# A routed expert layer behind an attention layer: GpSimd's stores in pairs, and three pieces of work in another place

## The chip, the core and the metric

The kernel runs on one core of a Trainium2 chip. A core has five engines that run their own instruction streams and meet only at semaphores: TensorE (PE; PEld is its weight load), VectorE (DVE), ScalarE (ACT), GpSimd (POOL) and SyncE (SP). The metric is the device time of one execution, in microseconds. The kernel before takes 296.75 us, the median of 3 runs (296.5 to 297.4).

## The reference

Eight sequences of 512 tokens (4096 tokens, width 256) pass through two gated layers, in fp32:

```python
x = x + tanh(g_xattn) * attention(layernorm(x), ctx)     # 16 heads, 16x16 scores within each token
x = x + tanh(g_ffn)   * ffn(layernorm(x))
# ffn: logits = xf @ Wg + bg ; idx = argmax(softmax(logits))
#      h = gelu(xf @ W1[idx] + b1[idx]) ; out = h @ W2[idx] + b2[idx]    (8 experts, width 256)
```

Each token's row goes through exactly one of 8 experts, so the kernel sorts the rows by expert.

## The kernel before

**Attention.** The 4096 tokens are 32 tiles of 128 rows, worked in 16 pairs (`pairs`). Each `slot(k, ...)` is one pair: projections, scores, softmax, values and output on TensorE, with VectorE and ScalarE between. Two pairs are a batch of four tiles; `m` numbers the batches, `last_batch` is 7.

**Routing.** When a batch's rows are final (`residual`, `stats_1`, `stats_2` on VectorE, then the standard deviation's power `pow_x1` on GpSimd), VectorE picks each row's expert (`pick_1` to `pick_7`), TensorE counts ranks by small matmuls (`ranks`), VectorE turns ranks into row numbers (`read_ranks`, `place_1` to `place_3`; the last of them casts to `pos_i`), and GpSimd scatters the four tiles to `routed_rows` in DRAM by four indirect DMAs (`route_tile`, line 1409; below: *routes*). 16 pairs are 32 routes on the semaphore `routed`, 16 counts each.

**Experts.** The sorted rows are read back in 39 blocks (`blocks`) of 128 rows. Block b passes, on every engine in order of b:

- SP `fetch`: reads the block's first row from a table, then loads it (`xb_in`), into a ring of 8; it waits until block b - 8 is finished. Blocks 0 to 15 (`EARLY`) hold rows of the batches placed first and come from a first table; blocks from 16 on need the second table (`tab_1` to `tab_10` on VectorE, spread over blocks 5 to 10) and all 32 routes (`routed`).
- VectorE `norm_b` (L1116), three blocks ahead; TensorE `transpose_b` (L640), two blocks ahead; ScalarE `copy_xbt` (L805) and the copy of the expert's first weights `copy_w1` (L790); TensorE `layer1` (L650, out to `ps_so` for even and `ps_tr` for odd blocks); ScalarE `gelu` (L798); TensorE `layer2` (L669, out to `ps_av` or `ps_to`); VectorE `finish` (L1133 adds the bias, frees the bank by `yb_done`; L1137 makes the output rows, `yf_done`); GpSimd `store` (L1465, an indirect DMA to `out_rows`, into a ring of 8 output tiles, semaphores `stored0` to `stored7`).
- The last three blocks (`AHEAD`) have the part of the output that doesn't need TensorE made beforehand (`prepare`, L1146) and then one instruction each (`finish_ahead`, L1157; two halves for the very last).

TensorE's slot for block b is `layer1(b)`, `layer2(b - 1)`, `transpose_b(b + 2)`.

**The seam.** While the last batch is still being routed, the first blocks already run. The order is written out by hand. On GpSimd: the two routes of batch 6, `pow_x1(15)`, the other two, the stores of blocks 0 to 2, two routes of batch 7, the store of block 3, two routes, and then only stores. On VectorE `end()` places batch 6 around the last `residual`; `pick_1(7)` waits for `pow_x1(15)`, and what stands behind it (the `finish` of block 1) waits too. On TensorE `ranks(7)` stands behind `layer2(4)`.

```python
def store(b, q, turn):
    ...
        wait_apart(pool, yf_done, b + 1, passed_pool)
    pool.indirect_dma_start(out, ... yf[j], None, bounds_check=limit, ...).then_inc(stored[j], 16)
```

A GpSimd wait holds back all that stands behind it on GpSimd; the instruction stream before has no wait there for an indirect DMA's landing.

## Time and profile before

| | |
|---|---|
| median of 3 runs | 296.75 us (296.5 to 297.4) |
| the profiled execution's own time | 295.98 us |
| its span, first to last instruction | 294.1 us |
| PE busy over the span | 277.9 us (94%) |
| DVE / ACT / POOL busy | 210.4 / 103.8 / 129.4 us |
| chain that ended last | PE 87%, DVE 3%, issue 2%, another core or an unknown queue 2% |
| indirect DMAs: routes, stores | 32, 39 |

The busy time of an engine is a sum over stages with different limits, so a change in one stage is read from that stage's rows. In the timelines a row is a start, a duration, the engine, the source line, the operation, what it writes and reads, and in square brackets the idle time of the engine before it with what ended it; "remote" there is a releaser that the profile does not tell. A POOL row of an indirect DMA is the time in which GpSimd makes its descriptors, not the transfer.

### The profile page before, as it was taken

What the parts mean: (1) busy time and instruction counts of PE and PEld (TensorE: products, weight loads), DVE (VectorE), ACT (ScalarE), POOL (GpSimd) and SP (SyncE); (2) the same over time, 40 slices, a digit from 0 to 9 for tenths busy, and PEclk for the clock granted to TensorE, in tenths of its full rate; (3) what the DMA queues carried; (4) which work ended last, traced back from release to release, by engine and by line L of the source; (5) the groups of instructions that cost most, each with busy time, mean ns of one, the idle gap of its engine ahead of it and who ended that gap; (6) DMA issues with size and microseconds to landing.
All of it is one profiled execution on the core that took longest, in us unless ns stands there. A gap on an engine that the chain in (4) does not pass through costs nothing.

```text
span 294.1 us, 9791 instructions
## 1 busy us (share of the span) xinstructions
PE 277.9 (94%) x3185; PEld 220.9 (75%) x3186; DVE 210.4 (72%) x613; ACT 103.8 (35%) x258; POOL 129.4 (44%) x156
## 2 busy tenths in 40 slices
PE   7999999999999999999999999899874799999994
PEld 6667777677677776776777768679763699999993
DVE  7667668786796786786877788698653666666664
ACT  2120321311303213113031131267451577777761
POOL 9613132152543624525427245413747254455455
PEclk9999999999999999999999999999999699999999
DMA  7866345476575764765746634332444244433410
GB/s 235 281 165 160 83 125 154 122 211 178 171 200 141 212 187 143 223 174 174 225 122 214 202 89 123 98 92 61 120 131 141 77 143 132 115 111 118 131 70 23
DMA packets 31240, 43.22 MB, mean 147 GB/s; under 512 B 7661, under 2 KB 18542, under 8 KB 31216
## 3 DMA queue, kind: packets, MB, share of 16 engines
q1 hardware_dynamic: 17760, 21.35, 26.7%
q10 hardware_dynamic: 10048, 12.99, 15.2%
q0 software_dynamic: 3408, 8.59, 8.2%
q8 instruction: 11, 0.18, 0.3%
q14 instruction: 13, 0.11, 0.1%
HBM read 24.83 MB, written 10.60 MB: 120 GB/s over the span
## 4 chain that ended last, share of the span: by engine, by line
PE 87%; DVE 3%; issue 2%; another core or an unknown queue 2%; DMA 2%; POOL 1%; ACT 1%; DVEq 0%; ACTq 0%; SPq 0%; POOLq 0%
PE ps_pr L409 18%; PE ps_qo L438 18%; PE ps_av L483 11%; PE ps_so L464 9%; PE ps_so L650 6%; PE ps_tr L650 5%; PE ps_to L669 5%; PE ps_av L669 5%; PE ps_tr L473 3%; PE ps_pr L640 3%; PE ps_to L496 2%; DMA sb_wqg<-wqg_in 2%; PE ps_pr L438 1%; PE ps_to L430 1%
## 5 line engine op out<-in xcount | busy, mean ns | idle before, releaser
L409 PE MATMUL ps_pr<-sb_wkv,sb_ct 128*128 128x512 f32 x120 | 57.7, 604 | 0.0
L723 ACT ACTIVATE sb_pe_x<-sb_pe_x 128x512 f32<-128x512 f32 x16 | 10.1, 631 | 111.5 <-DVE sb_pe_x L899 103.5
L1409 POOL DMA_INDIRECT routed_rows<-sb_xs,sb_pos_i x32 | 32.5, 1017 | 15.4 <-DVE sb_pos_i L1008 7.7
L1395 POOL TENSOR_SCALAR sb_ve<-sb_mv 128x2 f32<-128x2 f32 x16 | 3.5, 221 | 78.4 <-DVE sb_mv L858 75.9
L409 PEld LDWEIGHTS ps_pr<-sb_wkv,sb_ct 128*128 128x128 f32 x120 | 20.5, 190 | 17.7 <-issue 17.4
L483 PE MATMUL ps_av<-sb_vb,sb_at 128*32 128x128 f32 x1024 | 32.2, 274 | 1.1 <-issue 1.1
L464 PE MATMUL ps_so<-sb_kb,sb_y_q 128*32 128x128 f32 x1024 | 31.2, 273 | 0.1
L483 PEld LDWEIGHTS ps_av<-sb_vb,sb_at 128*32 128x32 f32 x1024 | 27.2, 110 | 5.0 <-issue 4.9
L438 PE MATMUL ps_qo<-sb_wog,sb_ot 128*128 128x264 f32 x120 | 29.6, 388 | 0.0
L438 PEld LDWEIGHTS ps_qo<-sb_wog,sb_ot 128*128 128x128 f32 x120 | 22.5, 190 | 9.2 <-issue 6.4
L438 PE MATMUL ps_qo<-sb_wqg_c,sb_xt 128*128 128x264 f32 x120 | 29.3, 387 | 0.0
L464 PEld LDWEIGHTS ps_so<-sb_kb,sb_y_q 128*32 128x32 f32 x1024 | 28.0, 110 | 1.6 <-issue 1.1
L790 ACT COPY sb_kb<-sb_w_all 128x514 f32 x39 | 24.2, 622 | 12.7 <-issue 12.7
L884 DVE STREAM_TRANSPOSE sb_y_q<-sb_q_n 128x512 f32<-128x512 f32 x16 | 17.4, 1091 | 15.6 <-ACT sb_q_n L718 15.6
L302 POOL TENSOR_TENSOR sb_cn<-sb_om,sb_rt 128x512 f32<-128x512 f32 x14 | 18.0, 1286 | 20.3 <-DVE sb_om L923 20.3
L1465 POOL DMA_INDIRECT out_rows<-sb_y_k,sb_tok_i x20 | 19.7, 983 | 16.3 <-issue 8.4
L650 PE MATMUL ps_so<-sb_ct,sb_kb 128*128 128x128 f32 x160 | 22.3, 284 | 4.4 <-ACT sb_ct L805 4.4
L438 PEld LDWEIGHTS ps_qo<-sb_wqg_c,sb_xt 128*128 128x128 f32 x120 | 21.7, 190 | 3.8 <-issue 0.5
L650 PEld LDWEIGHTS ps_so<-sb_ct,sb_kb 128*128 128x128 f32 x160 | 20.3, 198 | 4.9 <-issue 4.4
L669 PE MATMUL ps_to<-sb_w,sb_ht 128*128 x76 | 20.7, 397 | 2.5 <-DVE sb_yo L1133 1.3
L669 PE MATMUL ps_av<-sb_w,sb_ht 128*128 x80 | 20.4, 378 | 2.5 <-issue 2.0
L650 PE MATMUL ps_tr<-sb_ct,sb_kb 128*128 128x128 f32 x152 | 20.2, 276 | 0.0
(158 smaller groups left out, 493.9 us busy)
## 6 DMA issues: line engine op xcount, KB each, us to landing
sb_x<-x_in ACTq DMA_DIRECT2D x16, 256.0 KB, 3.5
sb_kb<-sb_y_k SPq DMA_DIRECT2D x124, 32.0 KB
sb_vb<-sb_y_v SPq DMA_DIRECT2D x120, 32.0 KB
sb_ct<-ctx_in ACTq DMA_DIRECT2D x14, 256.0 KB, 3.2
sb_xt<-xt_in_ ACTq DMA_DIRECT2D x14, 256.0 KB, 4.3
sb_xb<-routed_rows SPq DMA_DIRECT2D x25, 134.0 KB
sb_w_all<-w_in_ SPq DMA_DIRECT2D x4, 514.0 KB
sb_w<-w_in SPq DMA_DIRECT2D x4, 512.0 KB
```

The source lines that it names most:

```text
L302: eng.tensor_tensor(cn[:].rearrange("p u h i -> p h u i"), om[:].rearrange("p h (u i) -> p h u i", u=2), rt[:].rearrange("p (u i) -> p u i ...
L409: last = pe.matmul(pr[:, s * 512:(s + 1) * 512], lhsT=ct[i][:, kc, s, :], rhs=wkv[:, :, kc, :], start=(kc == 0), stop=(kc == KC - 1))
L438: last = pe.matmul(dst[:, s * 512:s * 512 + DE], lhsT=src[:, kc, s, :], rhs=w[:, kc, :], start=(kc == 0), stop=(kc == KC - 1))
L464: last = pe.matmul(so[32 * q:32 * q + 32, r * P:(r + 1) * P], lhsT=y_q[:, 4 * q + r, u:u + 2, :].rearrange("p a b -> p (a b)"), rhs=kb[i][ ...
L483: last = pe.matmul(av[32 * q:32 * q + 32, r * P:(r + 1) * P], lhsT=at[:, 4 * r + q, u:u + 2, :].rearrange("p a b -> p (a b)"), rhs=vb[i][: ...
L650: last = pe.matmul(h_ps[i][:, ic * P:(ic + 1) * P], lhsT=w1_sb[q % W1_RING][:, kc * D + ic * P:kc * D + (ic + 1) * P], rhs=xbt[i][:, kc, : ...
L669: last = pe.matmul(dst, lhsT=ht[i][:, ic, :], rhs=w2_sb[:, bass.ds(ex, 1), ic, first:end].rearrange("p a d -> p (a d)"), start=(ic == 0), ...
L723: act.activation(pe_x[:], pe_x[:], ACT.Exp, scale=float(H) ** -0.5).then_inc(exp_done, 1)
L790: act.copy(w1_sb[q % W1_RING], w1_all[:, bass.ds(ex, 1), :].rearrange("p a f -> p (a f)")).then_inc(w1_done, 1)
L884: dve.transpose(y_q[:, :, 0:3:2, :].rearrange("p a u i -> p i u a"), q_n[:].rearrange("p s (h i) -> p i s h", h=H)).then_inc(yq_out, 1)
L1409: pool.indirect_dma_start(rows, bass.IndirectOffsetOnAxis(ap=row_numbers(batch)[:, c:c + 1], axis=0), rows_of(j)[:, s, :], None).then_inc( ...
L1465: pool.indirect_dma_start(out, bass.IndirectOffsetOnAxis(ap=tok_i[j][:, 0:1], axis=0), yf[j], None, bounds_check=limit, oob_is_err=False). ...
```

## The change

Five edits. (1) GpSimd: all four routes of batch 7 stand behind the store of block 3, with a wait for `routed` behind the second and the fourth; behind the store of every other odd block up to 35 GpSimd waits until the store before it has landed. (2) VectorE: `place_2` and `place_3` of batch 6 stand ahead of the last `residual`. (3) TensorE: `ranks(7)` stands ahead of `layer2(4)`. (4) VectorE: `prepare` of the last block stands right behind that of block 36, in a buffer of its own (`y_q`). (5) TensorE: blocks 2 to 15 are written out and blocks 16 to 31 run in a loop of 8, where there were two loops of 4; the small matmul for `lap_ps` follows block 14 instead of 13.

```diff
+YL_ORDER = (0, 2, 1)
...
             slots(pe, pre, slot, end)
-            def slots_4(first, turns):
-
-                with pe.Fori(0, turns) as turn:
-                    for k in range(first, first + W1_RING):
-                        expert_slot(W1_RING * turn + k, k % W1_RING, turn)
-
-            for b in range(2, 6):
+            for b in range(2, EARLY):
                 if b == 5:
                     layer1(5, 5, 0)
-                    layer2(4, 0)
                     pe.wait_ge(res_step, 3 * last_pair + 1)
                     ranks(last_batch)
+                    layer2(4, 0)
                     transpose_b(7, 1)
                 else:
                     expert_slot(b, b % RING, b // RING)
-            slots_4(6, 2)
-            pe.wait_ge(lap_done, 1)
-            pe.matmul(lap_ps, lhsT=ones[:], rhs=lap_d[:], start=True, stop=True).then_inc(lap_spread, 1)
-            slots_4(14, 5)
-            for b in range(34, blocks + 1):
-                expert_slot(b, b % RING, b // RING)
+                if b == RING + 6:
+                    pe.wait_ge(lap_done, 1)
+                    pe.matmul(lap_ps, lhsT=ones[:], rhs=lap_d[:], start=True, stop=True).then_inc(lap_spread, 1)
+            block_slots(pe, expert_slot, 1)
...
+            def yl(b):
+
+                return y_q[:].rearrange("p a b h -> p (a b h)")[:, 0:D] if b == blocks - 1 else yo[b % 2][:]
+
             def prepare(b):
...
-                dve.wait_ge(yf_done, b - 1)
+                if b < blocks - 1:
+                    dve.wait_ge(yf_done, b - 1)
                 dve.wait_ge(stored[j], 16 * (b // OUT))
-                dve.scalar_tensor_tensor(yo[i][:], b2_sb[...
+                dve.scalar_tensor_tensor(yl(b), b2_sb[...
...
             def finish_ahead(b):
...
-                dve.wait_ge(yl_done, b - (blocks - AHEAD) + 1)
+                dve.wait_ge(yl_done, YL_ORDER.index(b - (blocks - AHEAD)) + 1)
...
                 place_1(m)
+                place_2(m)
+                place_3(m)
                 residual(n + 1, (n + 1) % 4)
-                place_2(m)
                 stats_1(n + 1, (n + 1) % 4)
-                place_3(m)
                 stats_2(n + 1, (n + 1) % 4)
...
-                if known and blocks - AHEAD <= b < blocks:
+                if known and blocks - AHEAD <= b < blocks - 1:
                     prepare(b)
+                if known and b == blocks - AHEAD:
+                    prepare(blocks - 1)
...
             for b in range(EARLY):
                 store(b, b % RING, b // RING)
-                if b in (2, 3):
-                    route_nth(last_batch, 2 * b - 4)
-                    route_nth(last_batch, 2 * b - 3)
-            block_slots(pool, store, 0)
+                if b == 3:
+                    for i in range(4):
+                        route_nth(last_batch, i)
+                        if i % 2 == 1:
+                            pool.wait_ge(routed, 32 * pairs - 16 * (3 - i))
+                elif b % 2 == 1:
+                    pool.wait_ge(stored[(b - 1) % OUT], 16 * ((b - 1) // OUT + 1))
+            def store_in_twos(b, q, turn):
+                store(b, q, turn)
+                if isinstance(b, int) and b >= blocks - 3:
+                    return
+                if q % 2 == 1 and isinstance(b, int):
+                    pool.wait_ge(stored[q - 1], 16 * (turn + 1))
+                elif q % 2 == 1:
+                    wait_apart(pool, stored[q - 1], 16 * (turn + 1), passed_pool)
+
+            block_slots(pool, store_in_twos, 0)
```

The first place is GpSimd's stream at the seam. `routed_rows` DMAs are routes (from `sb_xs_0` batch 6, from `sb_xs_1` batch 7), `out_rows` DMAs are stores; the number at the end of `sb_tok_i` is the block. Before:

```order
L1409 DMA routed_rows<-sb_xs_0,sb_pos_i 33792x268 x2
L1465 DMA out_rows<-sb_y_k_0,sb_tok_i_0 4096x256 [waits yf_done]
L1465 DMA out_rows<-sb_y_k_0,sb_tok_i_1 4096x256 [waits yf_done]
L1465 DMA out_rows<-sb_q_n,sb_tok_i_2 4096x256 [waits yf_done]
L1409 DMA routed_rows<-sb_xs_1,sb_pos_i 33792x268 [waits pos_done]
L1409 DMA routed_rows<-sb_xs_1,sb_pos_i 33792x268
L1465 DMA out_rows<-sb_q_n,sb_tok_i_3 4096x256 [waits yf_done]
L1409 DMA routed_rows<-sb_xs_1,sb_pos_i 33792x268 x2
```

And after:

```order
L1411 DMA routed_rows<-sb_xs_0,sb_pos_i 33792x268 x2
L1467 DMA out_rows<-sb_y_k_0,sb_tok_i_0 4096x256 [waits yf_done]
L1467 DMA out_rows<-sb_y_k_0,sb_tok_i_1 4096x256 [waits yf_done]
L1467 DMA out_rows<-sb_q_n,sb_tok_i_2 4096x256 [waits stored0,yf_done]
L1467 DMA out_rows<-sb_q_n,sb_tok_i_3 4096x256 [waits yf_done]
L1411 DMA routed_rows<-sb_xs_1,sb_pos_i 33792x268 [waits pos_done]
L1411 DMA routed_rows<-sb_xs_1,sb_pos_i 33792x268
L1411 DMA routed_rows<-sb_xs_1,sb_pos_i 33792x268 [waits routed]
L1411 DMA routed_rows<-sb_xs_1,sb_pos_i 33792x268
L1467 DMA out_rows<-sb_y_k_1,sb_tok_i_4 4096x256 [waits routed,yf_done]
L1467 DMA out_rows<-sb_y_k_1,sb_tok_i_5 4096x256 [waits yf_done]
L1467 DMA out_rows<-sb_y_v_0,sb_tok_i_6 4096x256 [waits stored4,yf_done]
```

The store of block 3 has moved ahead of batch 7's routes, and waits on landings (`stored0`, `routed`, `stored4`) stand where there were none; no wait stands between the store of block 3 and the first two routes but the old one on `pos_done`.

The second place is the end of `end()` on VectorE. L992 to L1008 are `read_ranks` to `place_3` of batch 6, L934 is the last residual, L940 and L946 its statistics. Before:

```order
L992 TENSOR_TENSOR sb_rb<-ps_av,sb_base 128x32
L997 TENSOR_TENSOR sb_base<-ps_av,sb_base 128x8
L998 TENSOR_TENSOR sb_rb<-sb_rb,sb_oh_b 128x32
L934 SCALAR_TENSOR_TENSOR sb_xs<-ps_qo,sb_tg,sb_x 128x2x264
L1002 TENSOR_REDUCE sb_pos<-sb_rb 128x4
L940 BN_STATS sb_st<-sb_xs 128x6 x2
L1008 CAST sb_pos_i<-sb_pos 128x4
L946 BN_AGGR sb_xs<-sb_st 128x2 x2
```

And after:

```order
L987 TENSOR_TENSOR sb_rb<-ps_av,sb_base 128x32
L992 TENSOR_TENSOR sb_base<-ps_av,sb_base 128x8
L993 TENSOR_TENSOR sb_rb<-sb_rb,sb_oh_b 128x32
L997 TENSOR_REDUCE sb_pos<-sb_rb 128x4
L1003 CAST sb_pos_i<-sb_pos 128x4
L929 SCALAR_TENSOR_TENSOR sb_xs<-ps_qo,sb_tg,sb_x 128x2x264
L935 BN_STATS sb_st<-sb_xs 128x6 x2
L941 BN_AGGR sb_xs<-sb_st 128x2 x2
```

The cast that GpSimd's first two routes wait for no longer stands behind the residual.

The third place is the last three blocks on VectorE, from the output rows of block 35 (`sb_q_n`). Before:

```order
L1137 SCALAR_TENSOR_TENSOR sb_q_n<-sb_yo,sb_tg,sb_xb 128x256
L1143 TENSOR_LOAD sb_tab
L1143 ISA x2
L1146 ISA
L1146 SCALAR_TENSOR_TENSOR sb_yo<-sb_b,sb_tg,sb_xb 128x256
L1148 TENSOR_TENSOR sb_tok_i<-sb_xb,sb_skip 128x1
L1157 SCALAR_TENSOR_TENSOR sb_y_k<-ps_av,sb_tg,sb_yo 128x256
L1143 TENSOR_LOAD sb_tab
```

And after:

```order
L1132 SCALAR_TENSOR_TENSOR sb_q_n<-sb_yo,sb_tg,sb_xb 128x256
L1142 TENSOR_LOAD sb_tab
L1142 ISA x2
L1146 ISA
L1146 SCALAR_TENSOR_TENSOR sb_yo<-sb_b,sb_tg,sb_xb 128x256
L1148 TENSOR_TENSOR sb_tok_i<-sb_xb,sb_skip 128x1
L1142 TENSOR_LOAD sb_tab
L1142 ISA x2
L1146 ISA
L1146 SCALAR_TENSOR_TENSOR sb_y_q<-sb_b,sb_tg,sb_wkv 128x256
L1148 TENSOR_TENSOR sb_tok_i<-sb_wkv,sb_skip 128x1
L1157 SCALAR_TENSOR_TENSOR sb_y_k<-ps_av,sb_tg,sb_yo 128x256
```

One whole `prepare` (a register load from the table, two computing instructions) has moved ahead of the output rows of block 36 (L1157).

## Rows read from the trace of the kernel before

**Rows 1.** Busy us by stretch: PE, PEld, DVE, ACT, POOL; PEclk, DMA share, GB/s
```profile
203.00:215.00 12.00, 9.64 (x72) 8.58 (x70) 7.75 (x32) 6.18 (x16) 8.00 (x9) 1.00 0.34 104
215.00:225.00 10.00, 7.34 (x45) 6.33 (x46) 6.88 (x31) 4.45 (x12) 5.83 (x6) 1.00 0.46 137
225.00:235.00 10.00, 5.87 (x28) 5.04 (x27) 4.46 (x17) 3.52 (x10) 3.96 (x5) 0.66 0.24 79
...
245.00:285.00 40.00, 40.00 (x283) 36.84 (x282) 25.33 (x80) 30.58 (x82) 19.96 (x21) 1.00 0.38 114
```

**Rows 2.** Timeline of GpSimd at the seam: start, us, what
```profile
204.88 1.07 POOL L1409 DMA_INDIRECT routed_rows<-sb_xs,sb_pos_i  x1 [4.75 <-DVE sb_pos_i L1008]
...
208.49 1.07 POOL L1409 DMA_INDIRECT routed_rows<-sb_xs,sb_pos_i  x1 [0.19 <-issue]
...
213.73 0.98 POOL L1465 DMA_INDIRECT out_rows<-sb_q_n,sb_tok_i  x1 [0.30 <-issue]
217.65 0.97 POOL L1409 DMA_INDIRECT routed_rows<-sb_xs,sb_pos_i  x1 [2.94 <-DVE sb_pos_i L1008]
...
226.63 0.98 POOL L1465 DMA_INDIRECT out_rows<-sb_y_v,sb_tok_i  x1 [0.30 <-issue]
```

**Rows 3.** Timeline of TensorE at the seam
```profile
209.58 1.13 PE L669 MATMUL ps_to<-sb_w,sb_ht 128*128 x4 [1.33 <-DVE sb_yo L1133]
...
212.55 0.24 PE L536 MATMUL ps_qo<-sb_oh_b,sb_ones 128*128 128x32 bf16 x4
...
215.13 1.12 PE L669 MATMUL ps_to<-sb_w,sb_ht 128*128 x4 [1.16 <-issue]
...
220.11 1.03 PE L669 MATMUL ps_to<-sb_w,sb_ht 128*128 x4
220.97 0.38 PE L640 MATMUL ps_pr<-sb_cst,sb_ct 128*128 128x128 f32 x2
...
229.75 2.07 PE L650 MATMUL ps_so<-sb_ct,sb_kb 128*128 128x128 f32 x8 [4.13 <-ACT sb_ct L805]
```

**Rows 4.** Timeline of VectorE at the seam
```profile
201.67 0.18 DVE L998 TENSOR_TENSOR sb_rb<-sb_rb,sb_oh_b 128x32 f32<-128x32 f32 x1
...
203.90 0.15 DVE L1008 CAST sb_pos_i<-sb_pos 128x4 uint32<-128x4 f32 x1
...
208.33 0.19 DVE L958 TENSOR_TENSOR sb_lg<-sb_xs 128x32 f32<-128x32 f32 x1 [2.29 <-POOL sb_xs L1404]
...
211.85 0.19 DVE L987 TENSOR_TENSOR sb_oh_b<-sb_le,sb_lw 128x32 bf16<-128x32 f32 x1
...
215.90 0.19 DVE L992 TENSOR_TENSOR sb_rb<-ps_qo,sb_base 128x32 f32<-128x32 f32 x1 [2.69 <-remote]
...
229.30 0.42 DVE L1133 TENSOR_TENSOR sb_yo<-ps_to,sb_b 128x256 f32<-128x256 f32 x1 [5.93 <-remote]
...
232.85 0.20 DVE L1080 CAST sb_tab<-sb_tab_t 128x64 int32<-128x64 f32 x1
```

**Rows 5.** Timeline of ScalarE at the seam
```profile
229.25 0.37 ACT L805 COPY sb_ct<-ps_pr 128x256 f32<-128x256 f32 x1 [5.11 <-remote]
```

**Rows 6.** Chain of waits, steady stretch: start, us, what (two `transpose_b`)
```profile
259.53 0.22 PE ps_pr L640 x2
...
261.50 0.22 PE ps_pr L640 x2
```

**Rows 7.** Timeline of all engines at the end
```profile
287.61 0.48 DVE L1157 SCALAR_TENSOR_TENSOR sb_y_k<-ps_av,sb_tg,sb_yo 128x256 f32<-128x256 f32 x1
...
288.37 0.98 POOL L1465 DMA_INDIRECT out_rows<-sb_y_k,sb_tok_i  x1 [0.63 <-DVE sb_y_k L1157]
...
290.07 0.48 DVE L1146 SCALAR_TENSOR_TENSOR sb_yo<-sb_b,sb_tg,sb_wkv 128x256 f32<-128x256 f32 x1 [0.36 <-DVE sb_y_k L1157]
...
290.86 0.34 DVE L1157 SCALAR_TENSOR_TENSOR sb_y_v<-ps_tr,sb_tg,sb_yo 128x128 f32<-128x128 f32 x1
291.47 0.98 POOL L1465 DMA_INDIRECT out_rows<-sb_y_v,sb_tok_i  x1 [0.51 <-DVE sb_y_v L1157]
```

More of the change, by code:

```diff
@@ L1137, in finish @@
                 dve.scalar_tensor_tensor(yf[j], yo[i][:], tg[:, 1:2], xb[q][:, 0:D], ALU.mult, ALU.add).then_inc(yf_done, 1)
+            def yl(b):
+                return y_q[:].rearrange("p a b h -> p (a b h)")[:, 0:D] if b == blocks - 1 else yo[b % 2][:]
             def prepare(b):
-                i, j = b % 2, b % OUT
+                j = b % OUT
                 x_b = xb[b % RING]
                 ex = dve.value_load(tab[0:1, 1, b:b + 1], min_val=0, max_val=E - 1)
-                dve.wait_ge(yf_done, b - 1)
+                if b < blocks - 1:
+                    dve.wait_ge(yf_done, b - 1)
                 dve.wait_ge(stored[j], 16 * (b // OUT))
-                dve.scalar_tensor_tensor(yo[i][:], b2_sb[:, bass.ds(ex, 1), :].rearrange("p a d -> p (a d)"), tg[:, 1:2],
+                dve.scalar_tensor_tensor(yl(b), b2_sb[:, bass.ds(ex, 1), :].rearrange("p a d -> p (a d)"), tg[:, 1:2],
                                          x_b[:, 0:D], ALU.mult, ALU.add).then_inc(yl_done, 1)
@@ L1156, in finish_ahead @@
                     dve.wait_ge(y_done, b + nth + 1)
-                    last = dve.scalar_tensor_tensor(yf[j][:, first:end], src, tg[:, 1:2], yo[i][:, first:end], ALU.mult, ALU.add)
+                    last = dve.scalar_tensor_tensor(yf[j][:, first:end], src, tg[:, 1:2], yl(b)[:, first:end], ALU.mult, ALU.add)
                 last.then_inc(yf_done, 1)
```

## The prediction, made blind

> **What bounds the kernel now.** I read the busy time by stretch first, to see where TensorE, the bound of most of the span, is not busy; then the timelines of the engines at that place; then the chain of waits; then the end.
>
> From 245 to 285 us TensorE is busy for 40.00 of 40.00 us, at the full clock [rows 1]. A block costs it 1.97 us there, from one transposition to the next (261.50 - 259.53) [rows 6]. Nothing done to other engines in that stretch can bring anything. The stretch from 203 to 235 us is another matter: TensorE is idle for 2.36, 2.66 and 4.13 us of its three parts, 9.15 us in all, and in the last part its mean clock is 0.66, that is, part of it at the lower of its two levels, 1.2 GHz, after the long idle time [rows 1]. (1 - 0.66) x 10 x 2 = 6.8 us of it were at half clock. I put 4.0 of them behind 229.75, where TensorE works again (layer 1 of block 10 takes 2.07 us [rows 3], more than a whole block in the steady stretch): work of 2.0 us that takes 4.0, another 2.0 us. So the seam loses 11.1 us, and 285.6 us would be the time without any of it (296.75 - 11.1). The reader is to see three separate losses in it.
>
> *Loss 1, 1.33 us.* Layer 2 of block 3 starts at 209.58, released by VectorE's bias addition [rows 3]. That one stood behind `pick_1(7)`, which waited 2.29 us for GpSimd's power (208.33) [rows 4], which stood behind two routes that started at 204.88 [rows 2], 0.83 us after their row numbers were cast (203.90 + 0.15) [rows 4]. The cast stood behind the last residual.
>
> *Loss 2, about 1.7 us.* TensorE finished the ranks of batch 7 at 212.79 by its rows [rows 3], but VectorE, which had waited 2.69 us for them, read them at 215.90 [rows 4]. TensorE itself waited 1.16 us at 215.13 [rows 3] for a gelu that was late in the same way, and some 0.5 us a slot later.
>
> *Loss 3, 8.2 us.* It is the same thing, larger. Layer 2 of block 7 was done at 221.14 and the transposition of block 10 at 221.35 [rows 3], but VectorE went on with the one at 229.30 and ScalarE with the other at 229.25, after idle times of 5.93 and 5.11 us that end with "remote" [rows 4, 5]. TensorE had nothing more it could do and stood 4.13 us until 229.75 [rows 3]; the rest of the idle time (9.15 - 1.33 - 1.16 - 0.5 - 4.13 = 2.0 us) was at block 8 in the same stretch, and the 2.0 us of half clock belong to it.
>
> So in losses 2 and 3 TensorE's work was done and its announcements reached the others 3 and 8 us late. What stands beside both is GpSimd: from 208.49 to 214.71 it issued 5 indirect DMAs, and from 217.65 to 227.61 8 of them, 0.30 us apart [rows 2]. In the steady stretch there are 21 of them in 40 us [rows 1], one a block, with about 1 us between, and TensorE never waits. I take the dense issue for the cause. The rows show that the two go together, not how.
>
> **The change part by part.**
>
> *Row numbers ahead of the last residual.* `place_2` can start at 201.85, when L998 is done [rows 4], and the cast ends about 0.4 us later, at 202.25, in a gap in which VectorE waits for TensorE anyway; 1.80 us earlier than 204.05. The routes start at 203.1, the power ends at 206.5 instead of 208.3 and so does the wait of `pick_1(7)`. Layer 2 of block 3 can then follow its predecessor at 208.25: the 1.33 us go, with 0.5 us to spare. Bounds: 0 (something else late there) to 1.8. I take 1.3.
>
> *Ranks ahead of layer 2 of block 4.* Removed from their way is one layer 2, 0.87 us. Added is a wait: one-hot rows were ready at 212.04 (211.85 + 0.19) [rows 4], and layer 1 of block 5 was done at about 211.7 (212.55 less a layer 2 [rows 3]), so TensorE would wait 0.35 us, with layer 2, its store and all later blocks behind it; the five small matmuls cost 0.1 us in either place. With the previous edit VectorE is 1.2 us earlier at this point, and the wait shrinks. Bounds: -0.5 to +0.1 us; I take -0.1.
>
> *Waits on GpSimd.* The last store is issued at 291.47 [rows 7], and the span ends at 294.1: an indirect DMA lands at most 2.63 us after its start. Two issues take 0.98 + 0.30 + 0.98 = 2.26 us, so the wait for the first of a pair costs at most 0.4 us by itself. But GpSimd then starts again only after 0.28 us (VectorE's rows at 288.09, the store at 288.37) [rows 7] to 0.83 us (above). A pair takes up to 2.63 + 0.83 = 3.46 us, with a pause of 0.6 to 1.2 us, where it took 2.56 with 0.30. Two blocks take TensorE 3.94 us: in the steady stretch the wait is free. Behind batch 7's routes the second of each pair is waited for too, a pause of 2.63 - 0.98 + 0.83 = 2.5 us, twice. The eight DMAs of loss 3 thereby become pairs: at the most two in a row. I expect that TensorE's announcements pass in the pauses, as they did around the pair at 204.88.
>
> What stays dense: routes 3 and 4 of batch 6 and the stores of blocks 0 and 1 are still four in a row, and so are the stores of blocks 2 and 3 with the first two routes of batch 7, if their row numbers are there. So I leave loss 2 as it is (0; bounds +1.7, all gone, and -1.7, doubled), and of loss 3 leave one stall of 2.0 us, the size of loss 2: 8.2 - 2.0 = 6.2 us gained, bounds 0 and 8.2.
>
> What is late next: batch 7's routes. With the numbers 4 us earlier (ranks not held up for 3 us, 1.3 from the first edit) the last one is issued about 222 and landed about 224.5; SP's fetch of block 16 then waits for it. Unheld, block 16 reaches TensorE's layer 1 at about 231 (12 slots of 1.97 behind block 4, in whose slot layer 2 of block 3 stands at 208.25) and must be normalised by 228: it is covered by 3 us, if the table, cast at 232.85 [rows 4] behind loss 3, comes some 8 us earlier, as all of VectorE does. The stores run late by up to 9 us then and gain 0.5 us a pair on TensorE; 8 output tiles allow 8 x 1.97 = 15.8 us less the landing.
>
> A page of the Trainium skill speaks of the price of such a wait: "DMA: Bandwidth & Descriptors", section "Anatomy of one DMA", has about 2.0 us of fixed time for a GpSimd DMA plus bytes over 436 GB/s, an estimate of 2.3 us for 128 rows of 1 KB. By it a wait for the first of a pair would be over as the second is issued, and the pause would be the restart alone.
>
> *The last block's preparation ahead.* One `prepare` moves ahead of block 36's output rows. It takes about 1.3 us of VectorE's path (register load, 0.48 and 0.15 us). From 286 us VectorE is nearly dense, so block 36's rows come about 1.0 us later than 288.09, and those of the last block, which today wait for the preparation at 290.07 [rows 7], gain at most 0.55 us. GpSimd then has three stores to issue 1.28 us apart: 289.1 + 0.27 + 2 x 1.28 = 291.9 instead of 291.47. A loss of 0.4 us; bounds -0.8 to +0.5.
>
> *Loops.* TensorE runs the same matmuls; 16 slots instead of 28 run in a loop. Steady slots with and without a branch cost 1.97 us, so 0.
>
> Sum: 1.3 - 0.1 + 0 + 6.2 - 0.4 = 7.0 us. The sum is made in the profiled execution, 295.98 us (294.1 of span and 1.9 around it), which stands 0.8 us under the median; the losses are differences and carry over. 296.75 - 7.0 = 289.7 us.
>
> **The rivals.**
>
> *A, all of losses 2 and 3 goes.* The pauses let every announcement through. For it: no late one in 40 us of steady issue. Against: four in a row remain twice. 289.7 - 1.7 - 2.0 = 286.0 us.
>
> *B, the pauses do nothing.* What holds TensorE's announcements is the number of DMAs worked off, not their spacing, or something else at that place. For it: the rows show no mechanism. Then only the first and the small terms are left: 296.75 - 1.3 + 0.1 + 0.4 = 295.95, within a measurement of no change.
>
> *C, slower: held until GpSimd has caught up.* If announcements are held for as long as GpSimd has indirect DMAs waiting, the pauses lengthen the hold. Batch 7's group was 8 x 1.28 = 10.2 us long; in pairs, with the store of block 3 ahead, it is 1.3 + 3.46 + 3.46 + 3.46 + 1.0 = 12.7 us. TensorE stands 2.5 us longer, at half clock after it: 295.95 + 2.5 = 298.5 us. It decides if TensorE still idles when GpSimd is between pairs.
>
> *D, the loop, not the pauses.* TensorE's 4.13 us begin where it branches back to block 10, and end with ScalarE's copy [rows 3]; against it, the branches between 245 and 285 us cost nothing [rows 1]. Gone with its half clock, 4.1 + 2.0, and the other terms as in B: 295.95 - 6.1 = 289.85 us. The Trainium skill ("Runtime: NRT & Kernel Launch", section "Instruction fetch mechanics") says that a taken branch out of the fetched window waits for a fetch; by that rule the gap would be one. The trace agrees neither in the steady branches nor in what ended the gap.
>
> **How the numbers follow.** Forecast (287.5 to 292.5 us): 0.44. A: 0.17. B: 0.18. C: 0.16. D: 0.05. The range reaches from 285.0, where A would lie with a better end, to 297.8, which leaves out most of C and little else. A measurement of this kernel can tell about 0.3%, 0.9 us, from no change. Faster: forecast, A, D and a small part of B, 0.69; same: the rest of B, 0.14; slower: C and a little of B, 0.17.
>
> **What would show each step.** First edit: GpSimd's first route of the group at about 203.1, and layer 2 of block 3 without idle time before it. Ranks: at most 0.5 us of wait ahead of them. Pauses: gaps of 0.6 us and more behind every second store at the seam, no idle time of VectorE or ScalarE over 3 us that ends with "remote", and TensorE's clock at 1.00 from 225 to 235. End: the store of block 36 later, the last one not earlier. The forecast is wrong if those idle times are still there although GpSimd pauses (B, C), or if SP waits for `routed` while TensorE idles at block 16.

## The result, and the profile after

The changed kernel takes 291.62 us (median of 6 runs, 290.77 to 293.15), the kernel before 296.84 us beside it (6 runs, 296.07 to 297.4): a ratio of 0.9837, 95% interval 0.9816 to 0.9859. The forecast was 289.7 us: right in direction and within the range, 1.9 us too low. The profiled execution took 290.77 us (span 288.9). Later sets of runs add what no single chip shows: on two of the four chips that they ran on, no trace has the losses 2 and 3 that the change goes for. Here and below a time is the median of all runs of a kernel and a ratio is that of its fast runs alone, so the two differ a little where slow ones fell in (1 to 3 of the runs with pauses to block 15, with threes, and with edit 2 or edit 4 undone).

The busy times by stretch, as [rows 1] (PE, PEld, DVE, ACT, POOL busy, PE's clock, DMA share, GB/s):

```profile
203.00:215.00 12.00, 11.03 (x81) 9.92 (x80) 9.41 (x38) 7.90 (x21) 7.99 (x9) 1.00 0.39 115
215.00:225.00 10.00, 8.23 (x56) 7.20 (x56) 7.65 (x34) 5.53 (x16) 4.94 (x5) 1.00 0.43 137
225.00:235.00 10.00, 10.00 (x73) 9.23 (x73) 7.52 (x27) 7.35 (x21) 6.20 (x6) 1.00 0.43 124
```

TensorE idles for 2.7 us of this stretch instead of 9.15, and is never at its lower clock. GpSimd's timeline answers to [rows 2]:

```profile
202.75 1.07 POOL L1411 DMA_INDIRECT routed_rows<-sb_xs,sb_pos_i  x1 [3.06 <-DVE sb_pos_i L1003]
...
210.54 0.99 POOL L1467 DMA_INDIRECT out_rows<-sb_y_k,sb_tok_i  x1 [0.30 <-issue]
213.72 0.98 POOL L1467 DMA_INDIRECT out_rows<-sb_q_n,sb_tok_i  x1 [2.19 <-DMA out_rows<-sb_y_k,sb_tok_i]
215.01 0.99 POOL L1467 DMA_INDIRECT out_rows<-sb_q_n,sb_tok_i  x1 [0.30 <-issue]
216.30 0.97 POOL L1411 DMA_INDIRECT routed_rows<-sb_xs,sb_pos_i  x1 [0.30 <-issue]
217.57 0.96 POOL L1411 DMA_INDIRECT routed_rows<-sb_xs,sb_pos_i  x1 [0.30 <-issue]
220.31 1.06 POOL L1411 DMA_INDIRECT routed_rows<-sb_xs,sb_pos_i  x1 [1.77 <-DMA routed_rows<-sb_xs,sb_pos_i]
221.68 0.96 POOL L1411 DMA_INDIRECT routed_rows<-sb_xs,sb_pos_i  x1 [0.31 <-issue]
225.05 0.99 POOL L1467 DMA_INDIRECT out_rows<-sb_y_k,sb_tok_i  x1 [2.41 <-DVE sb_y_k L1132]
...
278.33 0.98 POOL L1467 DMA_INDIRECT out_rows<-sb_y_k,sb_tok_i  x1 [1.08 <-issue]
```

The pauses are there. Two of them (2.19 and 1.77 us) follow four DMAs in a row. The row of 225.05 names VectorE as what ended the pause, but that release was long past; the wait for the fourth route is behind it. TensorE's, VectorE's and ScalarE's rows answer to [rows 3 to 5]:

```profile
207.73 1.09 PE L670 MATMUL ps_to<-sb_w,sb_ht 128*128 x4
...
210.29 0.18 PE L535 MATMUL ps_qo<-sb_oh_b,sb_tri 128*128 128x40 bf16 x1 [0.36 <-DVE sb_oh_b L982]
...
219.96 1.16 PE L651 MATMUL ps_tr<-sb_ct,sb_kb 128*128 128x128 f32 x8 [1.34 <-ACT sb_ct L800]
```

```profile
212.62 0.19 DVE L987 TENSOR_TENSOR sb_rb<-ps_qo,sb_base 128x32 f32<-128x32 f32 x1 [0.97 <-remote]
```

```profile
210.91 0.37 ACT L800 COPY sb_ct<-ps_pr 128x256 f32<-128x256 f32 x1 [2.09 <-remote]
```

Layer 2 of block 3 has no idle time ahead of it, the ranks waited 0.36 us, and the longest idle time that ends with "remote" is 2.09 us where 5.93 stood. Lateness is left behind the second four in a row, though no row calls it remote: the transposition of 218.23 ends at 218.61, ScalarE copies it at 219.54, and TensorE waits 1.34 us for that copy (the row of 219.96). What is new is the end, which answers to [rows 7]:

```profile
280.51 0.48 DVE L1157 SCALAR_TENSOR_TENSOR sb_y_k<-ps_av,sb_tg,sb_yo 128x256 f32<-128x256 f32 x1
...
281.02 0.98 POOL L1467 DMA_INDIRECT out_rows<-sb_q_n,sb_tok_i  x1 [0.42 <-DMA out_rows<-sb_y_k,sb_tok_i]
...
281.82 0.61 PE L670 MATMUL ps_tr<-sb_w,sb_ht 128*128 x4
...
283.70 0.98 POOL L1467 DMA_INDIRECT out_rows<-sb_y_k,sb_tok_i  x1 [0.41 <-DMA out_rows<-sb_q_n,sb_tok_i]
...
285.62 0.35 DVE L1157 SCALAR_TENSOR_TENSOR sb_y_v<-ps_tr,sb_tg,sb_y_q 128x128 f32<-128x128 f32 x1 [1.03 <-remote]
286.27 0.98 POOL L1467 DMA_INDIRECT out_rows<-sb_y_v,sb_tok_i  x1 [0.31 <-issue]
```

The rows of block 36 are made at 280.99, but GpSimd issues their store at 283.70, 2.71 us later: it is still behind. It issues its last seven stores with pauses of at most 0.42 us, from 278.33 on, and TensorE's last announcement (the semaphore update that tells the others that its matmuls are done) is late again: its matmuls end at 282.43, and VectorE reads them at 285.62. The last store itself follows GpSimd's own store before it (0.31 us, "issue"); the rows that it stores are made at 285.97, just in time for it. In the kernel before, TensorE's last matmuls were these:

```profile
289.60 0.61 PE L669 MATMUL ps_tr<-sb_w,sb_ht 128*128 x4
```

So TensorE was through 290.21 - 282.43 = 7.8 us earlier, and from there to the last store it took 3.84 us instead of 1.26.

### The profile page after: what moved, and what is told of

The parts are those of the page before. It is cut to its first block, busy times and chain, and to the rows that moved or that the text cites. A ratio compares the mean times of both kernels' runs of the same rounds, so it can differ in the third digit from the quotient of the medians.

```text
span 288.9 us, 9745 instructions
## 1 busy us (share of the span) xinstructions
PE 275.6 (95%) x3185; PEld 219.2 (76%) x3186; DVE 211.3 (73%) x613; ACT 102.9 (36%) x258; POOL 130.4 (45%) x156
## 4 chain that ended last, share of the span: by engine, by line
PE 75%; issue 7%; POOL 5%; DVE 5%; DMA 5%; ACTq 1%; ACT 1%; POOLq 0%; DVEq 0%
PE ps_qo L439 18%; PE ps_pr L410 18%; PE ps_av L484 11%; PE ps_so L465 9%; POOL out_rows L1467 5%; PE ps_av L670 3%; PE ps_so L651 3%; PE ps_to L670 3%; PE ps_tr L474 3%; PE ps_tr L651 3%; PE ps_to L497 2%; PE ps_pr L641 2%; DMA sb_kb<-sb_y_k 2%; DMA out_rows<-sb_q_n,sb_tok_i 2%; DVE sb_kb L1279 1%
## 5 line engine op out<-in xcount | busy, mean ns | idle before, releaser
L1411 POOL DMA_INDIRECT routed_rows<-sb_xs,sb_pos_i x32 | 32.7, 1023 | 12.5 <-issue 7.4
L651 PE MATMUL ps_so<-sb_ct,sb_kb 128*128 128x128 f32 x160 | 21.2, 276 | 0.2 <-ACT sb_ct L800 0.2
L670 PE MATMUL ps_to<-sb_w,sb_ht 128*128 x76 | 20.0, 385 | 0.3 <-ACT sb_ht L793 0.2
L651 PEld LDWEIGHTS ps_so<-sb_ct,sb_kb 128*128 128x128 f32 x160 | 19.5, 192 | 0.5 <-ACT sb_ct L800 0.5
```

The lines of the kernel that those rows point to most:

```text
L651: last = pe.matmul(h_ps[i][:, ic * P:(ic + 1) * P], lhsT=w1_sb[q % W1_RING][:, kc * D + ic * P:kc * D + (ic + 1) * P], rhs=xbt[i][:, kc, : ...
L670: last = pe.matmul(dst, lhsT=ht[i][:, ic, :], rhs=w2_sb[:, bass.ds(ex, 1), ic, first:end].rearrange("p a d -> p (a d)"), start=(ic == 0), ...
L1411: pool.indirect_dma_start(rows, bass.IndirectOffsetOnAxis(ap=row_numbers(batch)[:, c:c + 1], axis=0), rows_of(j)[:, s, :], None).then_inc( ...
```

## The experiments

Each set of kernels ran on one chip beside the kernel before: the first four on chip A, the next four on chip C, two on chip B, the last two on chip D. Before took 296.2 us on A and 296.3 on B, but 283.7 on C and 284.0 on D. Times are compared within a set only, 5 rounds each (3 for the fourth). The chip of the first set, that of the result above, is not on record. No trace of the kernel before was kept on B, C or D: what is said of it there rests on its time and on the traces of the others.

| kernel | chip | us | ratio to before (95%) |
|---|---|---|---|
| pauses alone | A | 293.96 | 0.9915 (0.9881 to 0.9948) |
| loops alone | A | 296.41 | 1.0003 (0.9980 to 1.0025) |
| pauses to block 15 only | A | 295.78 | 0.9980 (0.9948 to 1.0011) |
| before, one store held | A | 303.23 | 1.0225 (1.0180 to 1.0270) |
| threes from block 16 | C | 287.84 | 1.0149 (1.0103 to 1.0195) |
| gaps, no waits | C | 283.92 | 1.0002 (0.9985 to 1.0018) |
| changed, edit 2 undone | C | 293.55 | 1.0308 (1.0252 to 1.0363) |
| changed, edit 4 undone | C | 291.07 | 1.0198 (1.0141 to 1.0254) |
| changed kernel again | B | 291.53 | 0.9833 (0.9804 to 0.9863) |
| gaps, again | B | 293.41 | 0.9894 (0.9863 to 0.9925) |
| changed, waits written out | D | 284.03 | 1.0020 (0.9996 to 1.0043) |
| changed, edit 1 undone | D | 283.01 | 0.9977 (0.9958 to 0.9995) |

**Pauses alone (edit 1).** 

> The kernel before with the first edit alone (GpSimd's routes of batch 7 behind the store of block 3, and its waits). Theory, the dense issue on GpSimd makes TensorE's announcements late: most of the gain is here, no idle time over 3 us that ends with remote; the first loss (1.3 us ahead of layer 2 of block 3) stays, so 292.5 to 293.5 us, and the stores end late as in the changed kernel. Rival, the loop: the branch at block 10 is still there, so TensorE stands 4 us at it and the time is 296 to 297 us.

```diff
-                if b in (2, 3):
-                    route_nth(last_batch, 2 * b - 4)
-                    route_nth(last_batch, 2 * b - 3)
-            block_slots(pool, store, 0)
+                if b == 3:
...
+                            pool.wait_ge(routed, 32 * pairs - 16 * (3 - i))
+                elif b % 2 == 1:
+                    pool.wait_ge(stored[(b - 1) % OUT], 16 * ((b - 1) // OUT + 1))
...
+            block_slots(pool, store_in_twos, 0)
```

293.96 us, 0.5 us above the expected range, with 225 to 235 us fully busy at the full clock, although TensorE's loop and its branch are as before. The loop is out. But GpSimd is the bound at the end, more than in the changed kernel: TensorE's last matmuls start at 283.17 and end at 283.78, and the last store starts 6.39 us later, at 290.17. Its first route had started 6.03 us behind the start of the power ahead of it (205.92 - 199.89), 4.26 us in the changed kernel (202.75 - 198.49).

```profile
199.89 0.48 POOL L1402 TENSOR_SCALAR sb_ve<-sb_xs 128x2 f32<-128x2 f32 x1 [2.72 <-DVE sb_xs L946]
...
205.92 1.07 POOL L1409 DMA_INDIRECT routed_rows<-sb_xs,sb_pos_i  x1 [4.74 <-DVE sb_pos_i L1008]
...
290.17 0.98 POOL L1465 DMA_INDIRECT out_rows<-sb_y_v,sb_tok_i  x1 [0.30 <-issue]
```

**Loops alone (edit 5).** 

> The kernel before with the fifth edit alone (TensorE's blocks 2 to 15 written out, the rest in a loop of 8; the ranks where they were). Theory of the dense issue: nothing, 296.1 to 297.5 us, with the idle times of 5 us in VectorE and ScalarE still there. Rival, the loop: they are gone, 290 to 291 us.

```diff
-            for b in range(2, 6):
+            for b in range(2, EARLY):
...
-            slots_4(6, 2)
...
-            slots_4(14, 5)
...
+            block_slots(pe, expert_slot, 1)
```

No difference, and the gap with its half clock is where it was. The edit is worth nothing, and the rule of the Trainium skill on branches ("Runtime: NRT & Kernel Launch", section "Instruction fetch mechanics") doesn't explain the gap.

```profile
225.00:235.00 10.00, 5.07 (x25) 4.71 (x26) 4.55 (x17) 3.82 (x11) 4.41 (x5) 0.66 0.29 92
```

**Pauses to block 15 only.** 

> The changed kernel without the waits behind the stores from block 16 on; those at the seam stay. GpSimd is about 9 us late there and now issues 1.28 us apart until it has caught up, some 13 stores or more, in a stretch in which TensorE was busy throughout. Theory, dense issue anywhere: TensorE stands 2 us or more between 232 and 260 us, and the 2.3 us that GpSimd's lateness costs at the end come back: about 293 us (290 to 296). Rival, only the place (the routes, the seam) makes announcements late: TensorE stays busy, and the end is earlier: 289.2 us.

```diff
-            block_slots(pool, store_in_twos, 0)
+            block_slots(pool, store, 0)
```

295.78 us: nearly all of the gain is lost, and no difference from before is left that is clear of noise. GpSimd, late from the seam, issues seven stores in a row, the first 1.52 us and the others 1.28 us ahead of the next, and the stall of the seam stands in the middle of the steady stretch (GpSimd, ScalarE, VectorE and TensorE in one timeline):

```profile
250.12 0.98 POOL L1467 DMA_INDIRECT out_rows<-sb_y_k,sb_tok_i  x1 [0.31 <-issue]
...
256.54 0.98 POOL L1467 DMA_INDIRECT out_rows<-sb_y_v,sb_tok_i  x1 [0.30 <-issue]
258.78 0.62 ACT L793 ACTIVATE sb_ht<-ps_so,sb_kb 128x128 f32<-128x128 f32 x2 [4.45 <-remote]
258.97 0.42 DVE L1128 TENSOR_TENSOR sb_yo<-ps_to,sb_b 128x256 f32<-128x256 f32 x1 [5.16 <-remote]
...
259.54 2.07 PE L670 MATMUL ps_av<-sb_w,sb_ht 128*128 x4 [5.02 <-ACT sb_ht L793]
```

**One store held in the steady stretch.** 

> The kernel before, with GpSimd's store of block 19 held until the output rows of block 22 are made, and its blocks from 16 on written out. GpSimd is then three to four blocks late in the middle of the steady stretch and issues about 9 stores 1.28 us apart. Theory, dense issue anywhere: TensorE stands 2 to 8 us between 262 and 285 us, where it was busy throughout, and the time is 299 to 305 us. Rival, only the place or the routes: nothing, 296.1 to 297.5 us.

```diff
-            block_slots(pool, store, 0)
+            for b in range(EARLY, blocks):
+                if b == 19:
+                    pool.wait_ge(yf_done, 23)
+                store(b, b % RING, b // RING)
```

303.23 us, 7.0 us slower. This is the kernel before with one added wait on GpSimd, no route near, and GpSimd's stores from block 16 on written out. It isn't a lack of output tiles: block 24, whose rows VectorE makes at 268.26, behind the stall, uses the tile of block 16, which was stored before the hold. Five dense stores later TensorE stands, at the place where [rows 1] have 40.00 of 40.00:

```profile
261.89 0.98 POOL L1465 DMA_INDIRECT out_rows<-sb_q_n,sb_tok_i  x1 [7.39 <-DVE sb_y_v L1137]
...
267.03 0.98 POOL L1465 DMA_INDIRECT out_rows<-sb_y_v,sb_tok_i  x1 [0.30 <-issue]
...
269.46 2.08 PE L650 MATMUL ps_tr<-sb_ct,sb_kb 128*128 128x128 f32 x8 [2.56 <-issue]
```

```profile
265.00:275.00 10.00, 7.44 (x33) 6.33 (x32) 3.90 (x12) 4.08 (x12) 4.57 (x6) 0.68 0.29 93
```

Dense issue on GpSimd is thereby shown as the cause, on chip A, and the place doesn't matter. That lateness of GpSimd alone doesn't do it is shown by the pauses, with which GpSimd is late too (8.0 us at block 16 in the changed kernel: rows at 240.12, store at 248.13) and TensorE goes on.

**Threes, and gaps in place of waits, on chip C.** 

> The changed kernel, with GpSimd waiting behind every third store from block 16 on (places 2, 5 and 7 of each eight) instead of every second. Theory, the end is bound by GpSimd's lateness and three in a row are few enough: 8 blocks take GpSimd about 14 us where pairs take 15.2 and TensorE 15.8, so it is some 2 us less late at the end: 290.0 us (289 to 291). Rival, three in a row already hold TensorE's announcements long enough: TensorE idles over 1 us somewhere between 235 and 275 us, and the time is 292 us or more.

```diff
-                if q % 2 == 1 and isinstance(b, int):
+                if q in (2, 5, 7) and isinstance(b, int):
```

> The changed kernel, in which GpSimd doesn't wait for landings behind the stores from block 4 on but writes 256 values a partition behind each (about 0.3 us), with the blocks from 16 on written out; the waits at the routes stay. The stores are then about 1.6 us apart without ever waiting for one to land. Theory, the spacing is what matters and 0.6 us between two is enough: no idle time over 2 us that ends with remote, GpSimd is in time at the end, 289 to 290.5 us. Rival, it is the landing that lets the announcements through (a train of DMAs of any such spacing holds them): TensorE idles 2 us or more once between 225 and 260 us, 294 to 297 us.

```diff
+            def gap(b):
+                if b > 4:
+                    pool.wait_ge(gap_done, b - 4)
+                pool.memset(vb[1][:].rearrange("p t f -> p (t f)")[:, 0:256], 0.0).then_inc(gap_done, 1)
...
+                if b >= 4:
+                    gap(b)
+            for b in range(EARLY, blocks):
+                store(b, b % RING, b // RING)
+                if b < blocks - 3:
+                    gap(b)
```

Neither question was answered, since this chip has nothing to tell them apart: before takes 283.7 us, and no row from 150 us on in the traces of the four kernels run here shows an idle time that ends with "remote", four DMAs in a row or not. The gaps cost nothing (283.92). The threes cost 1.5%: with the waits GpSimd issues its last store 5.8 us behind the end of TensorE's matmuls (283.62 - 277.84), for no gain.

**Edit 2 and edit 4 undone, on chip C.** 

> The changed kernel without the second edit (place_2 and place_3 of batch 6 behind the last residual again). Theory, GpSimd's chain of work from its routes of batch 6 to the last store sets the end: all of it is 1.3 to 1.8 us later, 292.9 to 293.4 us. Rival, the edit's worth is TensorE's loss ahead of layer 2 of block 3, and that is hidden behind GpSimd's lateness at the end: 291.6 us, no difference.

```diff
-                place_2(m)
-                place_3(m)
                 residual(n + 1, (n + 1) % 4)
+                place_2(m)
                 stats_1(n + 1, (n + 1) % 4)
+                place_3(m)
```

> The changed kernel without the fourth edit (the last block is prepared right ahead of its own output rows again). Theory, VectorE is not on the path at the end, since GpSimd issues the store of block 36 only 2.7 us after its rows are made: no difference, 291.2 to 292.0 us. Rival, the last block's rows wait for the preparation as before the change: 0.4 to 0.6 us slower.

```diff
-YL_ORDER = (0, 2, 1)
+YL_ORDER = (0, 1, 2)
...
-                if known and b == blocks - AHEAD:
-                    prepare(blocks - 1)
```

293.55 and 291.07 us. The expected numbers were for a chip like A; here both must be read against 283.7. The second shows the end most plainly. TensorE is through at 277.88 (first row; PE busy 10.00 of 10.00 in each stretch from 215 to 275 us), and GpSimd goes on until its last store at 286.73, 8.9 us later:

```profile
277.27 0.61 PE L670 MATMUL ps_tr<-sb_w,sb_ht 128*128 x4
...
286.73 0.98 POOL L1464 DMA_INDIRECT out_rows<-sb_y_v,sb_tok_i  x1 [0.30 <-issue]
```

With the waits GpSimd alone sets the time there. It gets so late that VectorE waits for output tiles (1.48 us at 240.75, ended by a store's landing). Which of the two edits is worth more isn't shown. The ratios are 1.1% apart, but their intervals touch (from 1.0252, up to 1.0254), and the changed kernel itself was not run on this chip. Nor do the traces show the 1.8 us by which edit 2 starts GpSimd earlier: from the start of the power to the store of block 4 it takes 28.4 us without the edit (224.89 - 196.50) and 28.6 us with it (226.29 - 197.68), since GpSimd then waits 3.95 us for the landing of the last route with the edit, and 2.42 us without it.

**The changed kernel and the gaps, on chip B.** 

> The changed kernel itself, in another set. The kernel before took 296.2 to 296.8 us in two sets and 283.7 us in the third, so a set's chip decides whether announcements come late. Where before takes 296 us: 291.6 us again. Where it takes 284 us: TensorE has nothing to lose there, and the waits make GpSimd 7 us late at the end, as with the preparation back in its place: 290 to 292 us, 2% slower than before. Rival, the third set's kernels were slow for the parts taken back in them, not for the waits: 284 us there.

> The kernel with a gap of 0.5 us or more behind each store in place of the waits, in another set. Where before takes 296 us: by the theory that the spacing of 1.5 us is enough, 288 to 289 us, with GpSimd in time from about block 28 on; by the rival that announcements pass only where GpSimd waits for a landing, TensorE idles 2 us or more between 225 and 260 us, 293 to 297 us. Where before takes 284 us: 283.9 us again.

Chip B is like A: before 296.3, the changed kernel 291.53 as the first time. The gaps bring 1.1% where the waits bring 1.7%; the 288 to 289 us of the theory that 1.5 us between two starts is enough are missed. The rival isn't right either, since from 242 us on no announcement is late, though GpSimd waits for no landing. With a store every 1.48 us TensorE's announcements are late twice more behind the seam, while GpSimd is in time at the end:

```profile
229.70 0.98 POOL L1468 DMA_INDIRECT out_rows<-sb_y_v,sb_tok_i  x1 [0.17 <-issue]
230.67 0.34 POOL L1476 MEMSET sb_vb<- 128x256 f32 x1
231.18 0.98 POOL L1468 DMA_INDIRECT out_rows<-sb_y_v,sb_tok_i  x1 [0.17 <-issue]
...
233.45 0.42 DVE L1129 TENSOR_TENSOR sb_yo<-ps_to,sb_b 128x256 f32<-128x256 f32 x1 [3.32 <-remote]
...
240.28 0.42 DVE L1129 TENSOR_TENSOR sb_yo<-ps_to,sb_b 128x256 f32<-128x256 f32 x1 [3.05 <-remote]
```

So 0.5 us between two stores is too little there, and 1 us (the steady stretch of before) enough. Pairs with 0.9 us and more behind them are nearly enough: in the changed kernel's first trace TensorE is idle for 0.35 us between 235 and 265 us (9.74, 10.00 and 9.91 of 10.00).

**Waits written out, and no waits, on chip D.** 

> The changed kernel with GpSimd's blocks from 16 on written out, so that its waits are on constants; the waits are the same. In the kernel whose stores were held, written-out stores followed their rows by 0.3 us, looped ones by 0.8. Where before takes 296 us: each pair is 0.5 us shorter, GpSimd is in time for the last blocks and the late announcements there go too: 288.9 us (288 to 290). Rival, the shorter pauses let less through, and TensorE idles over 1 us behind 235 us: 291 to 294 us. Where before takes 284 us: GpSimd ends 2 to 4 us late instead of 7: 286 to 288 us, still slower than before.

```diff
-            block_slots(pool, store_in_twos, 0)
+            for b in range(EARLY, blocks):
+                store_in_twos(b, b % RING, b // RING)
```

> The changed kernel with the first edit undone (GpSimd's order as before, no waits), so edits two to five alone. Where before takes 296 us: only the first loss goes, the idle times that end with remote stay: 295.2 us (294.5 to 296.3). Where before takes 284 us: no announcement is late, and the two moves on VectorE and TensorE are all that counts: 282.5 us (282 to 283.3), the best there. Rival to both: the moves bring nothing without the waits, the same time as before.

```diff
-                if b == 3:
-                    for i in range(4):
...
+                if b in (2, 3):
+                    route_nth(last_batch, 2 * b - 4)
+                    route_nth(last_batch, 2 * b - 3)
+            block_slots(pool, store, 0)
```

Chip D is like C. Written out, the same waits cost nothing clear of noise (284.03), better than I expected: from 250 us on the idle time behind most pairs is 0.3 to 0.8 us (once 1.03; 0.42 in the second row below), and GpSimd, as late as in the other kernels at block 16, is nearly in time at the end.

```profile
269.60 0.98 POOL L1467 DMA_INDIRECT out_rows<-sb_y_v,sb_tok_i  x1 [0.30 <-DVE sb_y_k L1132]
271.00 1.23 POOL L1467 DMA_INDIRECT out_rows<-sb_y_k,sb_tok_i  x1 [0.42 <-DMA out_rows<-sb_y_v,sb_tok_i]
```

Without any waits, edits 2 to 5 bring 0.2% (0.05 to 0.4%), the best kernel on this chip. Its trace is the counterpart of the held store: 19 indirect DMAs in a row, none over 0.33 us behind the one before it, and TensorE doesn't notice:

```profile
204.46 1.07 POOL L1411 DMA_INDIRECT routed_rows<-sb_xs,sb_pos_i  x1 [0.19 <-issue]
...
227.89 0.98 POOL L1467 DMA_INDIRECT out_rows<-sb_y_k,sb_tok_i  x1 [0.33 <-issue]
```

```profile
215.00:225.00 10.00, 10.00 (x74) 9.24 (x73) 8.83 (x38) 7.47 (x20) 7.83 (x8) 1.00 0.56 176
225.00:235.00 10.00, 10.00 (x74) 9.23 (x73) 6.42 (x22) 7.59 (x20) 5.88 (x6) 1.00 0.53 161
```

## Why the prediction was right, and where it was off

*The cause.* "I take the dense issue for the cause" was an inference from two things side by side. The held store shows it (chip A, +7.0 us), and the kernel with pauses to block 15 shows it again. How dense issue does it stays open. What the prediction couldn't know is that it holds for one kind of chip: the "285.6 us without any of it" is near what before takes on C and D (283.7, 284.0). Most of what is missing between the two is a loss that the prediction overlooked, since it looked from 203 us on (the last section has its rows).

*The seam.* The terms 1.3 - 0.1 + 6.2 = 7.4 us are those of TensorE. It was through 7.8 us earlier, of which 0.36 us lie ahead of the seam (the power starts at 198.85 in before, 198.49 after): 7.4 us. Its parts: no idle time at layer 2 of block 3; 0.36 us at the ranks (at most 0.5 forecast); no half clock; and of the stalls, of which the forecast left 1.7 + 2.0 us, 2.4 us are there (0.61, 1.34 and 0.42 us; with the 0.36 us these are the 2.7 us of idle time), the largest at 219.96. TensorE's idle time would so make the gain 1.0 us larger than 7.4; small gaps behind 235 us and slower rows (layer 2 of block 4 takes 1.13 us) take that back, and I haven't followed them one by one.

*The end, the step that failed.* The forecast took 0.4 us off for it, by the preparation, and held that the stores, up to 9 us late, "gain 0.5 us a pair on TensorE". Even by these figures 16 pairs would gain 8.0 of the 9 us, so 1 us was missing from the sum. And the term behind them, "up to 2.63 + 0.83 = 3.46 us" a pair, was too small: from 225.05 to 278.33 the 14 pairs took 53.28 / 14 = 3.81 us each, 9 of them more than 3.46 and the longest 5.18 (239.24 to 244.42). Against TensorE's 3.94 they gained 0.13 us. The landings took longer than the end of before suggested: in the chain of waits three of them are 2.37, 2.87 and 3.33 us, and the longest pair leaves 4.9 us for one (5.18 less a restart of 0.31). The restart is only a small part: it takes 0.31 us where the wait is written out (283.70 - 283.39) and 0.97 in the loop (274.99 - 274.02), where the forecast allowed 0.83, and the six pairs that are written out (3.85 us each, 225.05 to 248.13) are no shorter than the eight of the loop (3.78, 248.13 to 278.33). GpSimd caught up as far as it did because TensorE was slower too, with its stalls left: from layer 2 of block 4 (211.17) to that of block 32 (270.55) it took 4.24 us for two blocks. So the lateness fell from 10.2 us at block 4 (rows at 214.82, store at 225.05) to 2.7 us at block 36, and the last stores came one behind the other. The end costs 3.84 - 1.26 = 2.6 us instead of 0.4. In the profiled executions this is the whole sum: 7.4 for the seam, less 2.6, and 0.36 from ahead of the seam give 5.2 us, which is what was measured, where the forecast had 7.4 - 0.4 = 7.0.

*The small terms.* The loops: 0, as forecast. Edit 2: the 1.3 us came on TensorE (no idle time ahead of layer 2 of block 3). At the end, which GpSimd sets, what counts is its earlier start: from the start of the power to the store of block 4 it takes 26.6 us (225.05 - 198.49), and 29.2 us with the pauses alone (229.11 - 199.89). Edits 2 to 4 together: the step from 0.9915 to 0.9833, 0.8% or 2.4 us, between two chips of the same kind and so not within one set. Where GpSimd isn't late (chip D) they bring 0.2%. Edits 2, 3 and 4 were not measured one by one on chips A and B.

*The rivals.* A fell: stalls behind four in a row are left, and at the end. B fell by the pauses alone, D by the loops alone. C's price fell, since GpSimd had stores waiting from 215 us to the end and the announcements passed all the same. Its idea fits the densest trains: in before, with the pauses to block 15, and with the held store ScalarE goes on only 2.0 to 2.6 us behind the start of the train's last store (229.25 - 226.63, 258.78 - 256.54, 269.04 - 267.03), when the stall has left GpSimd without rows. It doesn't fit the gaps on chip B, where VectorE goes on at 233.45 with GpSimd in the middle of nine stores.

*A better version.* None was shown for chips A and B. The pairs with waits written out might end earlier there, since GpSimd's lateness is what the end costs. But on chip D most of their pauses are 0.3 to 0.4 us from 250 us on, shorter than the 0.5 us that was too little on chip B, so they could as well bring the stalls back. It was not run on A or B.

## What to carry to other kernels

A wait put on an engine that is not the bound is paid at the end if the engine is late and gains little: multiply the gain a turn by the number of turns that are left. A cause read from two things side by side needs the experiment that makes the one and looks for the other; here one held store did it. And measure a fix for a stall of this kind on more than one chip: this change is worth 1.7% on two of them, and its waits, with one other edit undone, cost 2 to 3% on another.

## What the runs showed of the hardware

Chips differ. The same kernel takes 296.2 and 296.3 us on two and 283.7 and 284.0 on two others. It isn't the clock that they are granted: in every stretch up to 225 us it is 1.00 on all four, and below that only behind a stall or behind TensorE's last matmuls. On the first kind TensorE's announcements come 3 to 8 us late behind five to nine indirect DMAs of GpSimd issued up to 1.65 us apart, on the second not behind 19.

Four in a row are enough for a smaller loss. The routes of the earlier batches go out in twos, from 65 to 173 us, and TensorE is busy throughout (50.00 of 50.00 from 50 to 100 and from 100 to 150 us, 30.00 of 30.00 from 150 to 180). The first four in a row start between 181 and 183 us, in every kernel here. Behind them TensorE stands in the middle of its own matmuls on chips A and B and in the first set (PE is busy for 38.45 to 38.89 of the 40 us from 150 to 190), and not on C and D (39.95 or 39.96). In the kernel before, the first two rows are GpSimd's, the others TensorE's:

```profile
181.75 1.09 POOL L1409 DMA_INDIRECT routed_rows<-sb_xs,sb_pos_i  x1 [0.17 <-issue]
...
185.67 0.96 POOL L1409 DMA_INDIRECT routed_rows<-sb_xs,sb_pos_i  x1 [0.30 <-issue]
...
187.22 0.28 PE L483 MATMUL ps_av<-sb_vb,sb_at 128*32 128x128 f32 x1 [0.45 <-issue]
187.95 0.97 PE L483 MATMUL ps_av<-sb_vb,sb_at 128*32 128x128 f32 x26 [0.45 <-issue]
```

And the same 64 matmuls with the same four routes ahead of them on chip D, without waits:

```profile
184.56 1.95 PE L484 MATMUL ps_av<-sb_vb,sb_at 128*32 128x128 f32 x64
186.33 1.93 PE L465 MATMUL ps_so<-sb_kb,sb_y_q 128*32 128x128 f32 x64
```

From there to the same matmuls of the next pair it takes 9.76 us in before (194.82 - 185.06) and 7.76 on chip D (192.32 - 184.56): 2.0 us lost. With the losses 2 and 3 of the prediction, 1.7 + 8.2 us, that is 11.9 of the 12.5 us between chips A and C. The change leaves these four routes as they are; a pause between the second and the third is the next thing to try, and was not run.

At the seam, TensorE's matmuls are done by its rows, VectorE and ScalarE wait with "remote", and TensorE's own next instruction can stand too (2.56 us "issue" in the kernel with the held store). The Trainium skill warns that the end of a matmul's row is estimated, and that the semaphore goes out only when PSUM has acknowledged the writes ("Perfetto Trace Analysis", section "Tensor Engine Instruction (MATMUL, LD_WEIGHTS)"). That doesn't account for it: in the kernel with gaps on chip C VectorE reads the last bank but one 0.11 us behind the end of its matmuls' row,

```profile
275.74 0.71 PE L671 MATMUL ps_av<-sb_w,sb_ht 128*128 x4
...
276.56 0.35 DVE L1158 SCALAR_TENSOR_TENSOR sb_y_v<-ps_av,sb_tg,sb_y_q 128x128 f32<-128x128 f32 x1 [0.16 <-PE ps_av L671]
```

and the last one 0.04 us (276.90, 276.94), where in the changed kernel the same two took 2.25 us (281.99, 284.24) and 3.19. What carries the announcements so late, and why only on some chips, stays open.
